# Mixture-of-experts stage on one core: the next expert's weights in four shares instead of two bursts, and a second place for the activations' scratch rows

## What is computed

```python
sorted_xs = x_flat[xs_indices, :]                      # tokens sorted by expert, top 2 of 8
gate_out = jax.lax.ragged_dot(sorted_xs, w_gate, group_sizes=tokens_per_expert)
activation = jax.nn.gelu(gate_out[:, 0, :]) * gate_out[:, 1, :]
expert_outputs = jax.lax.ragged_dot(activation, linear, group_sizes=tokens_per_expert)
out = einsum('blkd,blk->bld', expert_outputs[xs_reverse_argsort], combine_weights)
```

## Time and profile before

| | |
|---|---|
| median of 3 runs | 2370.97 us (2370.23 to 2371.08) |
| the profiled execution | 2373.91 us, span 2372.1 us |
| mean granted TensorE clock | 0.954 of full speed |
| TensorE busy | 2165.7 us, 91% of the span |
| VectorE, ScalarE, GpSimd busy | 61%, 33%, 38% |
| HBM traffic | 404.88 MB, 171 GB/s over the span |
| phase 3 | from about 1150 us to the end |

### The profile page before, as it was taken

How to read it: one execution, slowest core, us unless ns; L and a number is a source line. 1 busy time by engine, 2 the same in 40 slices (tenths; PEclk the granted TensorE clock), 3 DMA queues, 4 the chain that set the end, 5 groups by cost and what they waited for, 6 DMA issues and landing times.

```text
span 2372.1 us, 43953 instructions
## 1 busy us (share of the span) xinstructions
PE 2165.7 (91%) x9280; PEld 1646.8 (69%) x9281; DVE 1451.2 (61%) x3341; ACT 774.5 (33%) x1395; POOL 892.8 (38%) x684
## 2 busy tenths in 40 slices
PE   7999999999888888886499998999989879989997
PEld 5688878888554445554388886887768768868886
DVE  6555555555488888887266664665646536656664
ACT  3244444444333333342123332332223213222332
POOL 5476665665256566675211111111111111111211
PEclk9999999999998899998799998999989989999998
DMA  7565555565444344556655556567676686575564
GB/s 236 206 228 191 205 170 202 165 212 189 160 143 167 137 180 175 182 204 241 220 130 129 130 132 204 125 129 185 154 206 130 166 248 131 128 216 127 129 130 85
DMA packets 292800, 404.88 MB, mean 171 GB/s; under 512 B 50126, under 2 KB 188366, under 8 KB 284878
## 3 DMA queue, kind: packets, MB, share of 16 engines
q1 hardware_dynamic: 164720, 257.57, 33.6%
q0 software_dynamic: 30640, 74.29, 15.4%
q10 hardware_dynamic: 97200, 70.82, 9.3%
HBM read 210.57 MB, written 191.98 MB: 170 GB/s over the span
## 4 chain that ended last, share of the span: by engine, by line
PE 29%; SPq 10%; issue 7%; DMA 5%; DVE 1%; ACTq 1%; ACT 0%; POOL 0%; DVEq 0%
PE bank L1800 29%; SPq L553 3%; DMA arow<-act_rows 3%; SPq L559 2%; SPq L560 2%; DMA act_rows<-hact 1%; SPq L551 1%; SPq L555 1%; DMA wbuf<-expert_split 1%; ACTq L1036 0%; SPq L531 0%; SPq L563 0%; SPq L562 0%; DVE gbr L1725 0%; ACT gb L1048 0%
## 5 line engine op out<-in xcount | busy, mean ns | idle before, releaser
L1800 PE MATMUL bank<-wbuf,x_t_hi 128*128 x2160 | 680.2, 397 | 63.7 <-DVE x_t_lo L1683 52.3
L779 POOL DMA_INDIRECT out_rows<-orow,cur_tok x135 | 209.0, 1548 | 1014.0 <-DVE orow L1728 944.9
L1800 PEld LDWEIGHTS bank<-wbuf,x_t_hi 128*128 128x128 f32 x2160 | 411.2, 191 | 160.6 <-issue 68.0
L1800 PE MATMUL bank<-wbuf,x_t_lo 128*128 x1080 | 427.6, 396 | 0.0
L1800 PE MATMUL bank<-wbuf,act_t_hi 128*128 x1080 | 347.2, 404 | 35.9 <-DVE act_t_lo L1700 18.0
L1689 DVE TENSOR_TENSOR hact<-bank,gact 128x512 f32<-128x512 f32 x135 | 93.3, 691 | 331.7 <-PE bank L1800 300.9
L1800 PEld LDWEIGHTS bank<-wbuf,act_t_hi 128*128 128x128 f32 x1080 | 209.2, 195 | 87.5 <-issue 40.4
L1800 PEld LDWEIGHTS bank<-wbuf,x_t_lo 128*128 128x128 f32 x1080 | 206.1, 191 | 43.5
L1800 PE MATMUL bank<-wbuf,act_t_lo 128*128 x540 | 217.8, 403 | 0.0
L1025 ACT ACTIVATE gact<-bank 128x512 f32<-128x512 f32 x135 | 80.7, 598 | 348.2 <-issue 215.3
L742 POOL DMA_INDIRECT expert_rows<-rows,dest x128 | 133.2, 1040 | 120.3 <-issue 65.0
(11 more groups left out here) (225 smaller groups left out, 4125.5 us busy)
## 6 DMA issues: line engine op xcount, KB each, us to landing
wbuf<-expert_split SPq DMA_DIRECT2D x24, 1536.0 KB
xrow<-expert_rows SPq DMA_DIRECT2D x540, 64.0 KB
act_rows<-hact ACTq DMA_DIRECT2D x135, 256.0 KB
arow<-act_rows ACTq DMA_DIRECT2D x540, 64.0 KB
expert_split<-split_hi SPq DMA_DIRECT2D x32, 768.0 KB, 3.5
expert_split<-split_lo SPq DMA_DIRECT2D x32, 768.0 KB, 5.8
xg<-in_x SPq DMA_DIRECT2D x16, 1024.0 KB, 5.4
q_rows<-qf SPq DMA_DIRECT2D x16, 1024.0 KB, 6.7
```

The costliest lines, as they stand in the source:

```text
L779: pool.indirect_dma_start(out=out, out_offset=bass.IndirectOffsetOnAxis(cur_tok[at][:, 0:1], 0), in_=orow[at % 2][:, :], in_offset=None, c ...
L1800: last = mm(dst, stationary(a, f), moving(b, f), start=(k == 0), stop=(k == parts * n - 1))
```

## The change

Instead of one burst of three parts and one of two, the parts are spread over the first four items of an expert: part 0 with the first, part 1 with the second, part 2 with the third, parts 3 and 4 with the fourth. If the expert ends before, what is left goes with its last item. Only expert 0's weights are loaded ahead; expert 1's come in shares with items 0 to 3. The first four steps (items 4 to 7) are written out, and the loop has one round fewer. The scratch rows have two places, taken in turn, so that `store_act(i)` waits for `act_back(i-2)`.

```diff
+SHARES = len(GATE_UP) + 1
...
-    ad = nc.dram_tensor("act_rows", (P, H), F32, kind="Internal").ap()
+    ad = nc.dram_tensor("act_rows", (2 * P, H), F32, kind="Internal").ap()
...
-        def next_weights(i, loaded, used, parts):
+        def next_weights(i):
 
             e = sp.value_load(tables[0:1, 1, bass.ds(i, 1)], min_val=0, max_val=E - 1)
+            e_after = sp.value_load(tables[0:1, 1, bass.ds(i + 1, 1)], min_val=0, max_val=E - 1)
             of_e = sp.value_load(tables[0:1, 2, bass.ds(i, 1)], min_val=0, max_val=ITEMS)
-            with sp.If(e > 0):
-                with sp.If(e < E - 1):
-                    with sp.If(of_e < 1):
-                        wait_apart(sp, loaded, 16 * len(parts) * (e + 1))
-                        wait_apart(sp, used, i)
-                        nxt = sp.value_load(tables[0:1, 1, bass.ds(i, 1)], min_val=0, max_val=E - 2) + 1
-                        for n in parts:
-                            load_weights(nxt, nxt & 1, n)
+
+            def share(k, used):
+                gate_up = k < len(GATE_UP)
+                parts = GATE_UP[k:k + 1] if gate_up else DOWNS
+                if k == 0:
+                    wait_apart(sp, s_wg, 16 * len(GATE_UP) * (e + 1))
+                if not gate_up:
+                    wait_apart(sp, s_wd, 16 * len(DOWNS) * (e + 1))
+                wait_apart(sp, s_u if gate_up else s_o, used)
+                nxt = sp.value_load(tables[0:1, 1, bass.ds(i, 1)], min_val=0, max_val=E - 2) + 1
+                for n in parts:
+                    load_weights(nxt, nxt & 1, n)
+
+            def shares_at(k):
+                share(k, i if k < SHARES - 1 else i - 2)
+                if k < SHARES - 1:
+                    with sp.If(e_after > e):
+                        for later in range(k + 1, SHARES):
+                            share(later, i)
+
+            with sp.If(e < E - 1):
+                with sp.If(of_e < 1):
+                    shares_at(0)
+                for k in range(1, SHARES if not isinstance(i, int) else min(SHARES, i + 1)):
+                    with sp.If(of_e > k - 1):
+                        with sp.If(of_e < k + 1):
+                            shares_at(k)
...
-        sp.wait_ge(s_wg, 16 * len(GATE_UP))
-        sp.wait_ge(s_wd, 16 * len(DOWNS))
-        for n in (*GATE_UP, *DOWNS):
-            load_weights(1, 1, n)
-
-        def weights_of(i):
-            if not isinstance(i, int) or i < ITEMS - 1:
-                next_weights(i, s_wg, s_u, GATE_UP)
-            next_weights(i - 1, s_wd, s_o, DOWNS)
+        next_weights(0)
 
         def step(i, at):
             load_rows(i, at)
-            weights_of(i - AHEAD)
-
-        with sp.Fori(0, (ITEMS - RING) // RING) as j:
+            next_weights(i - AHEAD)
+
+        for i in range(RING, 2 * RING):
+            step(i, i % RING)
+        with sp.Fori(1, ITEMS // RING - 1) as j:
...
-        def store_act(i):
-            wait_apart(act, s_ar, 16 * NBLK * i)
+        def store_act(i, at):
+            wait_apart(act, s_ar, 16 * NBLK * (i - 1))
             wait_apart(act, s_h, i + 1)
-            act.dma_start(ad[:, :], hact[:, :]).then_inc(s_hst, 16)
+            act.dma_start(ad[at % 2 * P:(at % 2 + 1) * P, :], hact[:, :]).then_inc(s_hst, 16)
```

More of the change, by code:

```diff
@@ L592, in _ @@
             step(i, i % RING)
-        for i in range(ITEMS - AHEAD, ITEMS):
-            weights_of(i)
+        for i in range(ITEMS - AHEAD, ITEMS - 1):
+            next_weights(i)
         sp.wait_ge(s_add, 16 * ITEMS)
@@ L1025, in gelu, with act_back @@
             act.activation(gact[:, :], G_B[:, :], ACT.Gelu_apprx_tanh).then_inc(s_ga, 1)
-        def store_act(i):
-            wait_apart(act, s_ar, 16 * NBLK * i)
+        def store_act(i, at):
+            wait_apart(act, s_ar, 16 * NBLK * (i - 1))
             wait_apart(act, s_h, i + 1)
-            act.dma_start(ad[:, :], hact[:, :]).then_inc(s_hst, 16)
-        def act_back(i):
+            act.dma_start(ad[at % 2 * P:(at % 2 + 1) * P, :], hact[:, :]).then_inc(s_hst, 16)
+        def act_back(i, at):
             wait_apart(act, s_ht, i)
@@ L1036, in act_back @@
                 act.dma_start(arow[b * BLK:(b + 1) * BLK, :].rearrange("i (a n) -> i a n", a=NBLK),
-                              ad[:, b * P:(b + 1) * P].rearrange("(a i) n -> i a n", a=NBLK)).then_inc(s_ar, 16)
+                              ad[at % 2 * P:(at % 2 + 1) * P, b * P:(b + 1) * P].rearrange("(a i) n -> i a n", a=NBLK)).then_inc(s_ar, 16)
         def act_hi(i):
@@ L1052, in _ @@
         x_hi(1, 1)
-        store_act(0)
+        store_act(0, 0)
         def item(i, at):
@@ L1059, in item @@
                 act_hi(i - 2)
-            act_back(i - 1)
+            act_back(i - 1, at - 1)
             gelu(i)
@@ L1063, in item @@
                 x_hi(i + 1, at + 1)
-            store_act(i)
+            store_act(i, at)
             if lagging:
@@ L1069, in _ @@
         act_hi(ITEMS - 2)
-        act_back(ITEMS - 1)
+        act_back(ITEMS - 1, ITEMS - 1)
         gb_rows(ITEMS - 2, ITEMS - 2)
```

## The result

The kernel with the change takes 2394.07 us (median of 6 executions, 2383.11 to 2398.52). On the same chip the kernel before takes 2370.60 us (6 executions, 2367.24 to 2373.42). The ratio is 1.0094, with a 95% interval of 1.0072 to 1.0116: **slower by 0.9%**, where I had forecast 2330.5 us and a gain of 1.7%. The time lies above my range (2302 to 2368), and it went by the rival to which I gave 0.13: SP's code decides. The profiled execution took 2398.52 us with a span of 2396.7 us, so its sums stand 4.5 us above the median: it is the longest of the six.

What follows compares the result with a forecast made beforehand. SP's stream, 8.62 us a step against TensorE's 8.24, was taken as the bound: 1121 - 20 + 11 + 0 + 15 = 1127 us puts the last rows at 2288.6; with 43.1 behind them the span ends at 2331.7. Forecast 2330.5 us, range 2302 to 2368.

Steps and rivals of the forecast that it cites:

- SP is the limit: Phase 3: SP's own work, 8.62 us a step against TensorE's 8.24, decides the time; 2315 to 2350 us, chance 0.50.
- rival C: SP's loop: code blocks needed faster than they come make the kernel slower, 2408 to 2597 us; chance 0.13.
- Net nothing: SP's loop code: second fetch wait gains 1.1 us a round, skipped code costs 1.1; bounds -40 and +62 us.
- my term for the branches: SP's step: eight branches in place of six, 40 ns each and up to 0.2 us with the jump, +0.5 us.
- -20 + 11 = -9 us: SP's work: one lookup fewer less two more branches, -20 us; the shares' own waits, lookups and issues, +11 us.
- SP's waits, 15 us: Waits SP must keep: some 3 us at the start, about 12 at the down weights of expert 5.
- What lies behind the last row load, 43.1 us: End of the span: 53.7 us before, 43.1 with the last rows only 4.94 us early in place of 15.5.
- I take the 50.4 us of the four places as removed: Bursts at four ordinary experts: shares remove TensorE's whole excess of 50.4 us; bounds for what stays 0 and 27.
- Rival D: Full DMA engines make each share meet the store, so 4 x 6.8 us stay; 2337 to 2366 us, chance 0.13.
- Worth nothing alone in ordinary items: Second place for scratch rows: no gain alone in ordinary items, only makes two shares in a row bearable.
- Expert 4: Short expert: the 11.4 us weights wait before expert 5 stays, the second burst's 11.6 us goes; bounds 3 and 17.
- The start: First items of phase 3: fewer weights in the first store's way gain 6.5 of 15.9 us; bounds 0 and 10.

Runs made afterwards that it cites:

- the lean kernel: The change with each load written once behind a short question, plus 42 loads a step that never run, against the kernel before: 0.9934.
- SP free: Kernel before, bursts kept, SP looking up the item's number within the expert first, all else behind one branch: 0.9998 with one place, 0.9903 with two.
- Lean shares: The change with each part's load written once, all behind one branch on the item's number within the expert, against the kernel before: 0.9907; with one place 0.9986.
- five lean shares: Each load written once behind the short question, two places, down parts split over the fourth and fifth items, against the kernel before: 2328.77 us, 0.9876.

## Why the prediction was wrong, point by point

**SP is the limit: right.** I said that SP would decide and not TensorE's side, and the marks I named for it came: SP's waits for VectorE all but vanish, VectorE's waits for rows appear, and about 8 fetches a round. My mark for rival C, over 35 us for four ordinary steps, is met in some rounds (35.8) and just missed in others (34.67). One more lookup (+2.3%) shows without any share that SP is the limit.

**SP's code, "Net nothing": the step that failed first.** I counted the same two waits a round and the skipped code at 1.1 us. It is three waits a round, and 206 us of them against 148: +58 us, near the end of my bound of +62. Another part is in the jumps: behind branches an ordinary step loses 0.86 us where it lost 0.5, which I had in my term for the branches. The never-taken code shows that the size of the code is a cause and not a companion: 25 us from it alone. It does not show every part of it. In the kernel before that code left the waits at two a round and made them and the jumps longer; in the lean kernel it brought nearly two more a round (31 gaps to 85). What decides between the two is open. The bound was right, and I chose within it by the row of one jump instead of by what I had said of this queue, that it has no reserve. The rest of SP's work was sized well enough: I forecast -20 + 11 = -9 us, and it was 1160.7 - 1121 - 58 = -18.

**SP's waits, 15 us: too low.** They are 24.5: 15.3 at the down weights of expert 5, where I had 12, and 9.2 us in four others, nearly all at the start, where I had 3.

**What lies behind the last row load, 43.1 us: too low.** It is 2396.7 - 2344.61 = 52.1. I had carried SP's lateness of the middle to the end, with the last rows 5 us early; they are 15.1 us early, for with the last expert SP's steps shorten to 7.89 us (items 112 to 132), which my sum by one mean step did not see. With these the sum closes: the span of 2331.7 that I forecast, + 48.7 own work (1160.7 for 1112), + 9.5 waits, + 9.0 at the end, - 2.2 for the earlier first load is 2396.7, the span measured. That it closes is arithmetic on the trace, not a further proof; the same 8.62 of before hid that its ordinary steps were 8.0 to 8.5, and those with a burst longer.

**"I take the 50.4 us of the four places as removed": the second step that failed**, and it would have failed with SP free too. Lean shares leave 8.1 us at items 36 to 40, more than the 6.8 of my bound for a place, 32.3 us at the four places together, more than the 27 of my bound for them, and 67 us over all of items 5 to 133, where the kernel before had 75. I had reasoned that a share can delay a transfer by its own 3.9 us at most, as if it had the engines alone. It has not: a share of 1.5 MB lands 8.1 us behind its issue (median of 21), and the read backs beside it land just after it. They took 6.5 and 9.35 us from their fourth issue where one needs 1.9, so the delay is 4.6 us beside a share of 3.9 and 7.5 us beside one of 5.2. By an estimate the ordinary traffic fills the gap: in 8.1 us it takes 0.59 x 8.1 = 4.8 us of the engines, and 4.8 + 3.9 is 8.7. The store, too, took 5.39 us in one and 3.24 in the other. Rival D had this mechanism, and held beside C. In the changed kernel itself the read backs close behind a share took 5.5 us in the median (21 of them), within my 4 to 8, but up to 9.7. Smaller shares shorten it to 3.9, so the size matters; the order of the packets and the ordinary traffic were not tried by themselves.

**"Worth nothing alone in ordinary items", the second place: true of the items, wrong as a price.** I gave it no term of its own. It is the one part that pays: 0.5% with the bursts, 0.8 to 1.0% where SP is free.

**Expert 4: half right.** The wait for the weights behind it stayed, as I said, but at 23.1 us instead of the 11.4 of before, above my mark of 6 to 17, since SP came to the third share late; with lean shares the longest such wait is 10.3 us. "The second burst's excess goes" failed: 9.2 us of it are there in the changed kernel's four items from 1937.62 on. With 25.3 at the first place that is 34.5 for the 24.9 of before, where I had 13.3.

**The start: right.** Item 2 begins at 1164.52 instead of 1172.44, 7.9 us earlier; I had 6.5. SP's later rows gave it back.

**The clock: half right, and worth nothing.** It is 0.91 to 0.95 at the four places instead of 0.78 to 0.90, where I had expected it near 1.00 in most of them, and TensorE waits in between for rows.

**The rule beside it.** The Trainium skill (Runtime: NRT & Kernel Launch, section Instruction fetch mechanics) calls the crossing of a block "mostly hidden". In this loop it is not: one of the three waits a round is the jump back, and the other two (1.26 and 1.61 us above) stand behind branches that skip code. I take them for blocks that came too late; the trace does not say which instructions a fetch brings. At the jump back the trace agrees with the other half of that rule, the wait for a page (3.36 us).

## What to carry to other kernels

Before adding branches and copies of code to a queue that issues loads in a loop, divide its own time per step by the step of the engine that it feeds: at 8.3 to 8.5 us against 8.24 even code that never ran cost 1%, and one lookup 2.3%. Ask the question that is mostly answered with no first, keep everything else behind it, and write each load once. And price a second buffer alone before pricing it as help for something larger: here it was the part that paid. A load's bytes say what it costs the engines, not how long it stands in the way of a small one: take its time from issue to landing for that.

## What the runs showed of the hardware

- Skipped code has a price on SP: 21 loads that never run in each of two questions took the fetches from 31 to 47 in 200 us and the kernel from 2371.6 to 2396.5 us. The loop with five lean shares needed no fetch at all in 200 us.
- A jump back waits longer while weights are in flight. In the changed kernel the gap is 5.88 us at 1476.34, with the DMA share at 0.81 from 1475 to 1483, and 3.36 us at 1849.91 between shares. Of its 84 gaps ten are over 4 us, up to 6.7. In the kernel before, the jump back waited 5.3, 7.0 and 5.3 us in the three rounds with the DMA share at 1.0 in the gap, and 2.4 to 2.9 in the rounds with it under 0.4.
- A small read back beside large loads is delayed by more than their bytes would take: 6.51 us beside a share of 1.5 MB and 9.35 us beside 2 MB, where it takes 1.9 us undisturbed. The added 4.6 and 7.5 us are more than the 3.9 and 5.2 us that the shares take by bytes, for a share of 1.5 MB is under way for 8.1 us, and the read backs landed 0.2 to 1.1 us after it.
- TensorE's clock stayed at 1.00 (the 2.4 GHz level) when TensorE stood idle for 1.0, 0.6 and 1.4 us in items 36, 37 and 38 with lean shares, and fell behind 2.05 us of it in item 40: 0.60 from 1479.50 to 1483.43. Here the small pieces of a stall cost less in clock than one large one, as the bursts' 0.73 and 0.79 show.
